# Batched one-hot comparisons in a graph kernel, and the basis product spread anew over its steps

## Chip, cores and metric

The kernel runs on one core of a Trainium2 chip. The metric is the device time of one execution in microseconds (us); less is better. A profile of one execution stands beside the timed runs; its span is a little shorter than the time of its own run.

## What is computed

625 nodes with 512 features pass through two graph blocks. The first is a graph convolution with batch norm, an exact GELU and a residual, then a layer norm; the second is a relational convolution of two layers with two relations, whose weights are sums over 30 basis matrices, then a residual and a layer norm. The edge list has 20,625 entries (src, dst, type), sorted by dst.

```python
# block 0: x -> layernorm(x + gelu(batch_norm(A_norm @ (x @ W0.T) + b0)) + x)
xw = x @ W.T
deg = segment_sum(ones_like(row), col)          # row, col: the edges and one loop for each node
dinv = where(deg > 0, rsqrt(deg), 0)
out = segment_sum((dinv[row] * dinv[col])[:, None] * xw[row], col) + b
# block 1: x -> layernorm(x + layer2(relu(layer1(x))))
def rgcn_gate_layer(x, row, col, edge_type, basis, att, gate_w, root, bias):
    w = einsum('rb,bio->rio', att, basis)       # basis: 30 x 512 x 512, fp32
    x_j = x[col]
    msgs[r] = (sigmoid(x_j @ gate_w[r]) * x_j) @ w[r]
    agg = segment_sum(where(edge_type == 0, msgs[0], msgs[1]), row)
    return agg + x @ root + bias
```

## The kernel before

All five engines run programs written out by hand, in program order, tied by semaphores; there is no scheduler. Products in fp32 precision are made of an upper and a lower part of each operand (`mm3`, three products at L476 to L478).

**The adjacency.** The edges are cut into 162 tiles of 128 edges, in 27 groups of 6. For a tile, `oh_src` (128 edges x place within a chunk of 125 nodes) and `oh_key` (128 edges x 160: five chunks, two relations, 16 columns of a window of destinations) are one-hot matrices, and TensorE multiplies them into `psE` (L570), three tiles to a window. VectorE makes the 162 `oh_key` (L1047) and 54 of the `oh_src` (L1045), one instruction for each tile with a scalar per edge; ScalarE makes the other 108 `oh_src` in two steps (L785, L791). VectorE then adds each of the 54 windows onto `B` (`add_window`, L1038) at a column that it reads from memory into a register (L1032). Group g waits on TensorE until the windows of group g - 2 are added, since `psE` has two halves. This loop over groups runs from 13.8 to 95.2 us. Behind it `AT` (B summed over relations, with the self loops added: L1103, L1105), the degrees (L601), `dinv`, and `z` (`xw` scaled, in two parts: L824, L1117) follow, then the aggregation `agg0` (L623) in eight steps (four blocks of 128 features, two halves of the nodes), batch norm and GELU by feature block, transposes back (`g`, L642), `residual_sum` (L1170) and layer norm, transposes of x1 (L650), the product with `root1`, then the gates, `Z` and `h` of each layer.

**The first product and the basis product in between.** `xw_part` (x @ W0.T) has 20 steps of three products; in the loop, groups 4 to 13 do two steps each. The combined weights are made from 64 basis parts (`basis_part`, L495), 32 for each layer. A part is four products of 128x32 by 128x512 on one slot of `basis_ring`, which has four slots of 1 MB; SP loads part n + 4 when part n has been used (L383). `basis_upto(n)` lets TensorE do the parts, in pairs, up to n. Eight parts make one block of weights (pp = 0 to 7), and each block goes through `w_first` (ScalarE, psW to `half`, L764, after part 8 pp + 3), `w_merge` (VectorE, L1011 to L1015, after part 8 pp + 7), `w_high` (ScalarE, L780) and `w_low` (VectorE, L1027). TensorE may not start part 8 pp + 8 before `w_first(pp)`, nor part 8 pp + 12 before `w_merge(pp)`. The numbers of parts done by places, before the change: 24 when the loop ends, 26 before `agg0`, 34 before the transposes `g`, 38 before `root1`, 46 after `root1`, 60 after Z of layer 1, 64 within `h`.

**Around the loop.** `w_merge(0)` stands at group 11, `w_low(0)` at 14, `w_merge(1)` at 20, `w_low(1)` at 23; `w_merge(2)` between `AT` and the degrees, `w_low(2)` in the third feature block of batch norm, `w_merge(3)` in the layer norm after the second chunk. `turned_low` (L1002) splits the nine transposed blocks of x and W0 in groups 1 to 5. `diag` (L1113) is made on VectorE and broadcast by TensorE (L611) into `dinv_b`, which VectorE copies (L1122).

## Time and profile before

| what | value |
|---|---|
| median of three runs | 326.71 us (326.15 to 327.0) |
| time of the profiled execution | 326.88 us |
| its span in the profile | 325.0 us |
| TensorE busy | 283.5 us, 87% |
| VectorE busy | 175.3 us, 54% |
| ScalarE busy | 135.3 us, 42% |
| GpSimd busy | 36.5 us, 11% |
| mean granted TensorE clock | 0.94 of full |
| moved by DMA | 73.7 MB |

Read with care: a matmul counts as busy until its modelled end, and the shares are averages over stages with different limits. Durations of consecutive VectorE instructions overlap a little, so that the distance of their starts is what an instruction costs in a row of them.

### The profile page before, as it was taken

To read this page: it belongs to the slowest core of one execution; us is meant where nothing else is said; L and a number is where in the kernel's file an instruction comes from. 1 tells how busy PE (TensorE), PEld (TensorE's weight loads), DVE (VectorE), ACT (ScalarE), POOL (GpSimd) and SP (SyncE) were. 2 spreads that over 40 slices of the span, in tenths; PEclk is the share of its full clock that TensorE was granted. 3 is DMA by queue.
4 is the path that set the end of the run, shared out by engine and by line. 5 is a ranking of instruction groups with operands and counts; after the bars stand their busy time and mean duration, and the time that the engine had idled before them with its cause. 6 is when DMAs were issued, how large, how long until landed. Compare 5 with 4: busy or idle time off the path is not lost.

```text
span 325.0 us, 4963 instructions
## 1 busy us (share of the span) xinstructions
PE 283.5 (87%) x1711; PEld 193.4 (60%) x1711; DVE 175.3 (54%) x538; ACT 135.3 (42%) x265; POOL 36.5 (11%) x71
## 2 busy tenths in 40 slices
PE   1768899885969999568999999999997999999991
PEld 1653455432336786424767656647795777787771
DVE  3878787999967847686310132233325125433333
ACT  4596868899701368647243114111313142100000
POOL 1001000000002900551000000000003600010000
PEclk9987999998695999779999999999998999999997
DMA  6974869599997999739998677975001400001112
GB/s 175 335 327 158 336 257 356 207 388 416 352 385 282 314 354 418 313 103 367 382 381 318 260 292 303 418 294 246 2 0 32 132 0 0 2 0 33 33 34 63
DMA packets 12759, 73.68 MB, mean 227 GB/s; under 512 B 1952, under 2 KB 2195, under 8 KB 4540
## 3 DMA queue, kind: packets, MB, share of 16 engines
q1 hardware_dynamic: 11282, 70.82, 57.4%
q0 software_dynamic: 1104, 2.36, 2.8%
q10 hardware_dynamic: 346, 0.17, 0.3%
q8 instruction: 14, 0.23, 0.3%
q14 instruction: 13, 0.11, 0.1%
HBM read 72.05 MB, written 1.28 MB: 226 GB/s over the span
## 4 chain that ended last, share of the span: by engine, by line
PE 61%; DVE 22%; issue 7%; DMA 4%; DVEq 2%; ACT 1%; POOL 1%; ACTq 0%; POOLq 0%
PE psW L495 13%; PE psM L476 10%; PE psM L477 9%; PE psM L478 9%; PE psM L717 6%; PE psM L737 6%; DVE oh_key L1047 4%; DMA basis_ring<-in_L_gnn_basis_dram 3%; PE psM L623 3%; DVE B L1038 2%; PE psE L570 2%; DVEq L1032 2%; DVE w L1027 1%; DVE x_sum L1170 1%; DVE AT L1103 1%
## 5 line engine op out<-in xcount | busy, mean ns | idle before, releaser
L495 PE MATMUL psW<-basis_ring,S 128*32 128x512 f32 x512 | 68.2, 651 | 3.2 <-DMA basis_ring<-in_L_gnn_basis_dram 3.1
L1217 DVE SCALAR_TENSOR_TENSOR zg<-psM,gate,zg 125x512 fp32r<-125x512 f32 x20 | 15.0, 751 | 59.5 <-ACT zg L891 59.5
L1047 DVE TENSOR_SCALAR oh_key<-iota_f,key 128x160 f16<-128x160 f16 x162 | 36.0, 262 | 2.6 <-PE psE L570 1.4
L785 ACT ACTIVATE oh_diff<-iota_f,edgeT 128x128 f16<-128x128 f16 x108 | 34.1, 389 | 3.4 <-DVEq L964 3.4
L495 PEld LDWEIGHTS psW<-basis_ring,S 128*32 128x32 f32 x512 | 13.9, 115 | 32.5 <-issue 26.4
L476 PE MATMUL psM<-w,hlT 128*125 128x512 f32 x80 | 33.1, 414 | 0.1
L891 ACT ACTIVATE zg<-psM,gate 125x512 fp32r<-125x512 f32 x20 | 13.8, 688 | 46.1 <-PE psM L478 45.7
L477 PE MATMUL psM<-w,hlT 128*125 128x512 f32 x80 | 32.3, 404 | 0.0
L478 PE MATMUL psM<-w,hlT 128*125 128x512 f32 x80 | 32.1, 402 | 0.0
L570 PEld LDWEIGHTS psE<-oh_key,oh_src 128*125 128x125 f16 x162 | 16.0, 150 | 25.2 <-issue 19.2
L570 PE MATMUL psE<-oh_key,oh_src 128*125 128x160 f16 x162 | 21.3, 261 | 10.2 <-issue 6.6
L717 PEld LDWEIGHTS psM<-BB,zg 125*128 125x128 f32 x160 | 23.1, 188 | 2.5 <-issue 1.7
L737 PE MATMUL psM<-zg,BB 125*125 125x512 f32 x100 | 24.0, 394 | 0.0
L717 PE MATMUL psM<-BB,zg 125*128 125x320 f32 (+1 forms) x160 | 23.8, 308 | 0.0
L791 ACT ACTIVATE oh_src<-oh_diff,ones_f 128x512 f16<-128x512 f16 x27 | 19.5, 722 | 7.1 <-PE psE L570 6.4
L737 PEld LDWEIGHTS psM<-zg,BB 125*125 125x125 f32 x100 | 18.6, 186 | 4.7
L1038 DVE TENSOR_TENSOR B<-B,psE 125x160 f32 x54 | 17.4, 322 | 6.8 <-issue 5.2
L476 PEld LDWEIGHTS psM<-w,hlT 128*125 128x125 f32 x80 | 15.1, 189 | 9.1 <-DVEq L1220 3.4
L460 POOL DMA_DIRECT2D root_raw<-in_L_gnn_root_dram x16 | 7.9, 501 | 101.0 <-DVE hlT L1243 101.0
L1027 DVE TENSOR_TENSOR w<-w_both,w 128x512 fp32r<-128x512 f32 x16 | 13.3, 869 | 9.9 <-ACT w L780 9.6
L478 PEld LDWEIGHTS psM<-w,hlT 128*125 128x125 f32 x80 | 15.3, 191 | 3.9
L477 PEld LDWEIGHTS psM<-w,hlT 128*125 128x125 f32 x80 | 15.3, 191 | 3.5
(159 smaller groups left out, 430.5 us busy)
## 6 DMA issues: line engine op xcount, KB each, us to landing
basis_ring<-in_L_gnn_basis_dram SPq DMA_DIRECT2D x64, 1024.0 KB, 7.1
root_raw<-in_L_gnn_root_dram POOLq DMA_DIRECT2D x32, 64.0 KB, 3.6
xs<-in_x_dram SPq DMA_DIRECT2D x1, 1120.0 KB
out_dram<-xs SPq DMA_DIRECT2D x5, 224.0 KB
w_raw<-in_L_gnn_W_dram SPq DMA_DIRECT2D x1, 1024.0 KB, 10.9
bias_b<-in_L_gnn_bias_dram POOLq DMA_DIRECT2D x1, 250.0 KB, 3.8
xs<-in_x_dram SPq DMA_DIRECT2D x1, 130.0 KB
out_dram<-xs SPq DMA_DIRECT2D x5, 26.0 KB
```

What stands on the lines that cost most here:

```text
L476: nc.tensor.matmul(o, l_hi, r_hi, start=start, stop=False)
L477: nc.tensor.matmul(o, l_hi, r_lo, start=False, stop=False)
L478: last[0] = nc.tensor.matmul(o, l_lo, r_hi, start=False, stop=stop)
L495: m = nc.tensor.matmul(psW[32 * j:32 * j + 32, cc % 2, :], S[:, cc % 2, cc // CH, q].rearrange("p k r -> p (k r)"), ring[:, n % RING, j, : ...
L570: nc.tensor.matmul(psE[0:PC, g % 2, at:at + KEYS], oh_src[:, g % 3, j * P:j * P + PC], oh_key[:, t % OH, :], start=(j % SG == 0), stop=(j ...
L717: last[0] = nc.tensor.matmul(bank(("h", f, h))[:, 0:n], zg[:, i, d, r, f * P:(f + 1) * P], BB[:, at:at + n], start=(d + r + i == 0), stop= ...
L737: last[0] = nc.tensor.matmul(bank(("out", c))[0:PC, :], BB[:, at:at + PC], zg[:, i, d, r, :], start=False, stop=(d == NC - 1 and r + i == 2))
L785: nc.scalar.activation(oh_diff[:, g % 3, j * P:(j + 1) * P], iota_f[:, 0:P], ACT.Abs, bias=edgeT[:, 0, g * G + j:g * G + j + 1], scale=-1. ...
L791: nc.scalar.activation(oh_src[:, g % 3, 0:GA * P], oh_diff[:, g % 3, :], ACT.Relu, bias=ones_f[:, 0:1], scale=-1.0).then_inc(src_ready, 1)
L1027: v.tensor_tensor(lo, full, hi, ALU.subtract).then_inc(w_lo, 1)
L1038: v.tensor_tensor(to, to, psE[0:PC, g % 2, h * KEYS:(h + 1) * KEYS] .rearrange("p (c t w) -> p c t w", c=NC, t=R), ALU.add).then_inc(win_a ...
L1047: v.tensor_scalar(oh_key[:, t % OH, :], iota_f[:, 0:KEYS], key[:, t:t + 1], None, ALU.is_equal) \
```

## The change

- **Comparisons in one instruction for six tiles.** `one_hots` compares a row of numbers with the edges' values laid out in pairs: each value stands twice, side by side (`place_pairs`, `key_pairs`, two casts before the loop), so that both inputs and the output are fp16 with an inner row of two. One instruction makes a group's six `oh_src` (6 x 126), one its six `oh_key` (960). ScalarE's share of `oh_src` is gone.
- **Register reads.** The two registers of a group's windows are read behind the two comparisons, and `add_window` follows for both windows of group g - 2.
- **Spreading.** In the loop, the xw steps run up to 2(g - 3)/3 and the basis parts up to 2g/3 - 2; 15 of the 20 steps and 16 parts lie in the loop, five steps behind it. The parts done are then 16 when the loop ends, 20 before `agg0`, 28 before `g`, 30 behind it, 36 before `root1`, 44 after `root1`, 58 after Z of layer 1, 64 within `h`.
- **The middle.** The self loops are written into `B` at the start by ScalarE and taken off the edge matrix again (`own_edge`) before `z_parts(0)`. `diag` is made by GpSimd, its broadcast products stand behind the first step of `agg0`, and ScalarE copies the result. `w_merge(1)` stands behind `z`, `w_low(1)` in the second feature block, `w_merge(2)` in the third, `w_low(2)` and `w_merge(3)` behind the first three chunks of x1, `w_high(2)` and `w_first(3)` ahead of the last GELU.
- **W0 in another row order.** W0 is loaded in four transfers so that h comes in the order of the basis product; the vectors are then needed in one order only.

```diff
-OH = 12
-GA = 4
+OH = 3 * G
+PLACES = PC + PC % 2
...
-        FIRST_XW = 4
+        PARTS_IN = 15
...
-        FIRST_AT = {8: 0, 17: 1}
-        HIGH_AT = {13: 0, 22: 1}
-        MERGE_AT = {11: 0, 20: 1}
-        LOW_AT = {14: 0, 23: 1}
+        MERGE_AT = {16: 0}
+        LOW_AT = {19: 0}
...
-            sp.dma_start(w0_raw[:], W0.rearrange("(c p) o -> p c o", p=P)).then_inc(w0_in, 16)
+            for j in range(JB):
+                sp.dma_start(w0_raw[32 * j:32 * j + 32], W0.rearrange("(k c j) o -> j k c o", k=2 * KB, c=KC)[j]) \
+                    .then_inc(w0_in, 16)
...
+            pool.wait_ge(dinv_ready, 1)
+            for c in range(NC):
+                nc.gpsimd.tensor_scalar(diag[:, c, :], ident[0:PC, 0:PC], dinv_p[:, c:c + 1], None, ALU.mult) \
+                    .then_inc(diag_ready, 1)
...
-                if FIRST_XW <= g < FIRST_XW + NC * KC // 2:
-                    xw_part(2 * (g - FIRST_XW))
-                    xw_part(2 * (g - FIRST_XW) + 1)
-                basis_upto(9 * g // 10)
+                xw_upto(2 * (g - 3) // 3)
+                basis_upto(min(2 * g // 3 - 2, PARTS_IN))
...
+            xw_upto(NC * KC)
             pe.wait_ge(vec_permuted, 1)
...
-            basis_upto(24)
...
-            basis_upto(25)
...
-            basis_upto(26)
+            basis_upto(17)
+
+            basis_upto(19)
...
+                    if (f, h) == (0, 0):
+                        pe.wait_ge(diag_ready, NC)
+                        for i, (c0, c1) in enumerate(((0, 4), (4, NC))):
...
-                basis_upto((28, 30, 31, 32)[f])
-            basis_upto(33)
+                basis_upto((21, 23, 25, 27)[f])
...
+            basis_upto(29)
...
-                basis_upto((35, 36, 37)[c])
+                basis_upto((31, 33, 35)[c])
...
-                    basis_upto(39 + KC * h + f)
+                    basis_upto((37, 37, 39, 39, 41, 41, 43, 43)[KC * h + f])
...
-                            basis_upto(47 + 7 * (R * c + r) // 5)
+                            basis_upto((45, 47, 47, 49, 51, 51, 53, 55, 55, 57)[R * c + r])
...
-                    basis_upto(min(60 + KC * h + f, 2 * CH * SUB - 1))
+                    basis_upto((57, 59, 59, 61, 61, 63, 63, 63)[KC * h + f])
...
+            def one_hots(out, pairs, first, n, width):
+
+                pair = iota_f[:, 0:width].rearrange("p (k i) -> p k i", i=2)
+                shape = [P, n, width // 2, 2]
+                return v.tensor_tensor(out, pair.unsqueeze(1).broadcast_to(shape),
+                                       pairs[:, first:first + n].unsqueeze(2).broadcast_to(shape), ALU.is_equal)
...
-                link(v.tensor_tensor(AT[:, c], B[:, c, 0, 0:N2], B[:, c, 1, 0:N2], ALU.add))
-                d = AT[:, c, c * PC:(c + 1) * PC]
-                v.tensor_tensor(d, d.bitcast(F32), ident[0:PC, 0:PC], ALU.add).then_inc(at_ready, 1)
-            w_merge(2)
+                v.tensor_tensor(AT[:, c], B[:, c, 0, 0:N2], B[:, c, 1, 0:N2], ALU.add).then_inc(at_ready, 1)
...
+            w_merge(1)
+            dve.wait_ge(dinv_b_ready, 2)
...
-                if f == 2:
-                    w_low(2)
...
+                if f == 1:
+                    w_low(1)
+                if f == 2:
+                    w_merge(2)
...
-                if c == 1:
-                    w_merge(3)
...
-            w_low(3)
+            w_low(2)
+            w_merge(3)
```

VectorE in the middle of the loop, the instructions of one group. Before (`TENSOR_LOAD` reads a window's register):

```order
L1045 TENSOR_SCALAR oh_src<-iota_f,edgeT 128x128
L1047 TENSOR_SCALAR oh_key<-iota_f,key 128x160
L1045 TENSOR_SCALAR oh_src<-iota_f,edgeT 128x128
L1047 TENSOR_SCALAR oh_key<-iota_f,key 128x160 x3
L1032 TENSOR_LOAD base_i
L1032 ISA x2
L1038 ISA
L1038 TENSOR_TENSOR B<-B,psE 125x10x16
L1047 TENSOR_SCALAR oh_key<-iota_f,key 128x160 x2
L1032 TENSOR_LOAD base_i
```

After, on the same engine at the same place:

```order
L1055 TENSOR_TENSOR oh_src<-iota_f,place_pairs 128x6x126
L1038 TENSOR_LOAD base_i
L1038 ISA x2
L1055 TENSOR_TENSOR oh_key<-iota_f,key_pairs 128x960
L1038 TENSOR_LOAD base_i
L1038 ISA x2
L1048 ISA
L1048 TENSOR_TENSOR B<-B,psE 125x10x16
L1048 ISA
L1048 TENSOR_TENSOR B<-B,psE 125x10x16
```

Eight comparisons have become two, and no comparison stands between the two windows any more.

TensorE in the loop, before (one group with two xw steps and a pair of parts, and the start of the next):

```order
L570 MATMUL psE<-oh_key,oh_src 125x160 x6
L476 MATMUL psM<-w0T_hi,xT_hi 125x512
L477 MATMUL psM<-w0T_lo,xT_hi 125x512
L478 MATMUL psM<-w0T_hi,xT_lo 125x512
L476 MATMUL psM<-w0T_hi,xT_hi 125x512
L477 MATMUL psM<-w0T_lo,xT_hi 125x512
L478 MATMUL psM<-w0T_hi,xT_lo 125x512
L495 MATMUL psW<-basis_ring,S 32x512 x8
L570 MATMUL psE<-oh_key,oh_src 125x160 x6
```

After, on TensorE, three groups:

```order
L580 MATMUL psE<-oh_key,oh_src 125x160 x12
L479 MATMUL psM<-w0T_hi,xT_hi 125x512
L480 MATMUL psM<-w0T_lo,xT_hi 125x512
L481 MATMUL psM<-w0T_hi,xT_lo 125x512
L498 MATMUL psW<-basis_ring,S 32x512 x8
L580 MATMUL psE<-oh_key,oh_src 125x160 x6
L479 MATMUL psM<-w0T_hi,xT_hi 125x512
L480 MATMUL psM<-w0T_lo,xT_hi 125x512
L481 MATMUL psM<-w0T_hi,xT_lo 125x512
```

Three groups now carry two xw steps and one pair of parts; before, two groups carried four steps and one pair.

VectorE behind the loop, before and after:

```order
L1103 TENSOR_TENSOR AT<-B 125x626
L1105 TENSOR_TENSOR AT<-AT,ident 125x125
L1011 SCALAR_TENSOR_TENSOR w_both<-psW,mask_h,w_half 128x512
L1013 SCALAR_TENSOR_TENSOR w_half<-psW,mask_h,w_half 128x512
L1015 STREAM_SHUFFLE w_both<-w_half 128x512
L1108 COPY deg<-psM 125x5
L1113 TENSOR_SCALAR diag<-ident,dinv_p 125x125 x5
L1117 SCALAR_TENSOR_TENSOR z<-xw,dinv_p,z 125x512 x5
```

```order
L1121 TENSOR_TENSOR AT<-B 125x626 x5
L1123 COPY deg<-psM 125x5
L1129 SCALAR_TENSOR_TENSOR z<-xw,dinv_p,z 125x512 x5
L1018 SCALAR_TENSOR_TENSOR w_both<-psW,mask_h,w_half 128x512
L1020 SCALAR_TENSOR_TENSOR w_half<-psW,mask_h,w_half 128x512
L1022 STREAM_SHUFFLE w_both<-w_half 128x512
```

The first two rows of before stand five times in turn; a `w_merge` that stood ahead of the copy of the degrees now stands behind `z`, and `diag` has left the engine.

## Rows read from the trace of the kernel before

**Rows 1.** Busy time by stretch: us, busy by engine, granted clock, DMA share, GB/s

```profile
13.80:37.20 23.40, 18.65 (x113) 12.08 (x112) 18.82 (x76) 19.32 (x49) 1.04 (x1) 0.85 0.69 267
37.20:62.40 25.20, 22.88 (x153) 13.69 (x152) 20.73 (x96) 20.68 (x49) 0.00 (x0) 1.00 0.82 317
62.40:95.20 32.80, 25.17 (x193) 10.42 (x193) 29.70 (x137) 23.75 (x57) 0.00 (x0) 0.90 0.92 356
...
95.00:101.00 6.00, 5.16 (x30) 5.13 (x30) 5.64 (x11) 0.22 (x1) 0.00 (x0) 0.62 0.99 418
...
138.00:146.00 8.00, 5.14 (x28) 1.84 (x28) 7.17 (x19) 3.40 (x5) 4.17 (x9) 0.79 0.29 92
...
149.70:172.70 23.00, 23.00 (x168) 16.46 (x169) 7.17 (x12) 8.85 (x17) 0.00 (x0) 1.00 0.98 376
172.70:217.00 44.30, 44.30 (x252) 26.91 (x253) 10.19 (x15) 11.62 (x19) 0.00 (x0) 1.00 0.78 307
```

**Rows 2.** Groups of instructions by line: count, busy us, mean ns, idle before

```profile
L1047 DVE TENSOR_SCALAR oh_key<-iota_f,key 128x160 f16<-128x160 f16 x162 | 36.0, 262 | 2.6 <-PE psE L570 1.4 <-DVE xT_lo L1002 0.7 <-DVE w0T_lo L1002 0.2
...
L1038 DVE TENSOR_TENSOR B<-B,psE 125x160 f32 x54 | 17.4, 322 | 6.8 <-issue 5.2 <-DVE B L1038 1.4
...
L1045 DVE TENSOR_SCALAR oh_src<-iota_f,edgeT 128x128 f16<-128x128 f16 x54 | 13.5, 250 | 0.6 <-DVE w_both L1015 0.5
...
L1103 DVE TENSOR_TENSOR AT<-B 125x626 fp32r<-125x626 uint16 x5 | 4.0, 806 | 0.9 <-DVE B L1038 0.9
```

**Rows 3.** Timeline of VectorE within the loop: start us, duration us

```profile
65.48 0.26 DVE L1045 TENSOR_SCALAR oh_src<-iota_f,edgeT 128x128 f16<-128x128 f16 x1
...
67.29 0.26 DVE L1045 TENSOR_SCALAR oh_src<-iota_f,edgeT 128x128 f16<-128x128 f16 x1
...
75.03 0.74 DVE L1011 SCALAR_TENSOR_TENSOR w_both<-psW,mask_h,w_half 128x512 f32<-128x512 f32 x1
...
77.46 0.26 DVE L1045 TENSOR_SCALAR oh_src<-iota_f,edgeT 128x128 f16<-128x128 f16 x1 [0.25 <-DVE w_both L1015]
...
83.26 1.95 DVE L1027 TENSOR_TENSOR w<-w_both,w 128x512 fp32r<-128x512 f32 x2
85.13 0.24 DVE L1045 TENSOR_SCALAR oh_src<-iota_f,edgeT 128x128 f16<-128x128 f16 x1
```

**Rows 4.** Timeline of VectorE at the end of the loop

```profile
93.97 0.33 DVE L1038 TENSOR_TENSOR B<-B,psE 125x160 f32 x1 [0.43 <-DVE B L1038]
95.19 0.81 DVE L1103 TENSOR_TENSOR AT<-B 125x626 fp32r<-125x626 uint16 x1 [0.89 <-DVE B L1038]
...
96.24 0.80 DVE L1103 TENSOR_TENSOR AT<-B 125x626 fp32r<-125x626 uint16 x1
```

**Rows 5.** Timeline of TensorE: a group of the loop, and the broadcast of dinv

```profile
45.35 0.58 PE L570 MATMUL psE<-oh_key,oh_src 128*125 128x160 f16 x6
...
47.28 1.92 PE L495 MATMUL psW<-basis_ring,S 128*32 128x512 f32 x16
49.14 0.63 PE L570 MATMUL psE<-oh_key,oh_src 128*125 128x160 f16 x6
...
105.59 1.88 PE L611 MATMUL psM<-diag,ones_f 125*128 125x125 f32 x10 [0.17 <-DVE diag L1113]
```

**Rows 6.** The chain that ended last, in order of time: start us, us

```profile
100.42 0.75 DVE w_both L1011
...
103.23 1.21 POOL dinv_p L430
104.47 1.06 DVE diag L1113 x5
105.53 3.32 DVE z L1117 x5
108.90 1.98 PE psM L623 x12
...
133.01 0.72 PE psM L642 x4
...
149.67 0.39 PE psM L476
```

More of the change, by code:

```diff
@@ L255, in gnn_block @@
         use("deg", "dve")
-        for h in range(2):
-            use(("dinv", h), "dve")
         NBB = -(-NC * R * NC // 4)
@@ L562, in _ @@
             for g in range(NG):
[L563 removed]
+                pe.wait_ge(key_ready, g + 1)
                 if g >= 2:
@@ L1058, in _ @@
[L1058 to L1063 removed]
+                    dve.wait_ge(b_zero, NC)
+                for i in TURNED_LOW_AT.get(g, ()):
+                    turned_low(i)
+                for i, w in enumerate(range(2 * (g - 2), 2 * (g - 1)) if g >= 2 else ()):
+                    add_window(w, at[i])
@@ L1112, in _ @@
             for c in range(NC):
-                last = v.tensor_scalar(diag[:, c, :], ident[0:PC, 0:PC], dinv_p[:, c:c + 1], None, ALU.mult)
-            last.then_inc(diag_ready, 1)
-            for c in range(NC):
                 dve.wait_ge(z_hi, c + 1)
@@ L1229, in z_parts @@
                             .then_inc(root_ready, 1)
+            for d in range(NC):
+                own_edge = BB[:, d * (R * NC + 1) * PC:(d * (R * NC + 1) + 1) * PC]
+                last = v.tensor_tensor(own_edge, own_edge.bitcast(F32), ident[0:PC, 0:PC], ALU.subtract)
+            link(last)
             z_parts(0)
```

165 lines of the change are left out of this document (80 added, 85 removed).

## Prediction

> **What bounds the kernel now.** I read the stretches first [rows 1]. A reader should see three regimes. In the loop, 13.8 to 95.2 us, no engine is full: VectorE is busy for 18.8 + 20.7 + 29.7 = 69.3 of 81.4 us, TensorE for 66.7. From 149.7 to 217 TensorE is busy without a gap, and up to 172.7 the DMA share is 0.98 too. Between them the limit passes from one engine to another: at 138 to 146 us DMA is busy for 0.29 of the time, since the ring is full and TensorE uses no parts. The costliest groups [rows 2] and the timeline [rows 3] then give the loop's prices. Starts of two like instructions are 1.81 us apart (65.48, 67.29): that is a group's bill on VectorE. A window lasts 0.32, but instructions in a row overlap by about 0.08 (the `w_low` from 83.26 lasts 1.95 and the next starts at 85.13), so it costs 0.24; two of them leave 1.34 us for the six keys and two places. TensorE [rows 5]: six adjacency products and two xw steps take 1.93 us (45.35 to 47.28), a pair of basis parts 1.86 (47.28 to 49.14). In groups 4 to 13, two groups with one pair cost TensorE 2 x 1.93 + 1.86 = 5.7 us against 3.6 on VectorE; later VectorE is the longer one. The two take turns, and nobody gets the sum of both evened out. That is what the spreading attacks.
>
> **The loop.** Removed: 162 + 54 comparisons on VectorE (1.34 us a group). Added: one of 756 elements and one of 960 a group. The trace has no two-input VectorE instruction with fp16 alone. Upper bound, the two-input rows: 160 elements take 322 ns, 626 take 806 [rows 2], so 1.04 ns an element and 156 ns fixed; the two take 0.94 + 1.15 less two overlaps = 1.92 us. Lower bound, the one-input fp16 rows: 128 columns take 250 ns and 160 take 262, 0.38 ns an element; that gives 0.78 us. I take half the upper bound's rate, 0.52 ns, because the inputs are two-byte as in the lower row and two as in the upper: 0.55 + 0.65 - 0.17 = 1.03 us.
> The Trainium skill (VectorE: DVE Perf Modes, section on the perf-mode tier table) says that a tensor_tensor gives two results a cycle where all operands are 16-bit with unit step in SBUF, and one otherwise; no run here shows it yet. By it the sum would be the 1.03, and the 1.92 if the broadcast pairs did not count as unit step.
> The rest, against 95.2 us, the start of `AT` [rows 4]:
> - two casts ahead of the first key, 324 outputs each at the upper rate: +0.8;
> - 27 groups x (1.34 - 1.03): -8.4;
> - the second window stands directly behind the first and has to wait for its end: 0.46 in place of 0.24, 25 times: +5.5. The register reads now run while a comparison of half a microsecond is worked on;
> - one `w_merge` (75.03 to 77.46, 2.43) and one `w_low` (83.26 to 85.13, 1.87) leave the loop [rows 3]: -4.3;
> - VectorE's idle time is 81.4 - 69.3 = 12.1 us. The last four windows and the read of `more` keep 2.2 (0.43 and 0.89 are shown in [rows 4]), the waits of nine `turned_low` on themselves another 2.2 (0.25 each). Of the other 7.7, which were waits for TensorE's bursts, for ScalarE's places and for register reads (5.2 of the 6.8 at L1038 [rows 2]), I keep 1.2: -6.5.
> Sum -12.9: `AT` starts at about 82.3 us; call it L. TensorE doesn't forbid it: three groups cost it 1.2 + 1.5 + 1.86 = 4.6 us (three times 0.4, two steps, a pair) against 3 x 1.73 = 5.2 on VectorE. ScalarE, busy for 19.3 + 20.7 + 23.8 = 63.8 us there [rows 1], loses the places, most of that, and so will be ready before it is asked. ScalarE's five copies onto B and the W0 load in four transfers I cost at nothing: the first hide before the first window, the second behind the first comparisons; if W0 came late, the first adjacency product, which stands behind a W0 transpose on TensorE, would move with it one for one.
>
> **From L to the end of root1.** Before, this took 95.2 to 172.7, 77.5 us. Eight parts fewer are done by L, and six of them must be done in this stretch. Two paths run through it, and the later one counts.
> *Engines.* Before the degrees' copy VectorE loses a 2.4 us `w_merge` (100.42, [rows 6]) and five adds (96.24 - 95.19 = 1.05 a chunk, 0.72 without). TensorE, though, has five xw steps to do first (3.6 us) and 25 small products; I expect the copy 4.8 us behind L, 7.6 before. The 1.06 us of `diag` leave the path (104.47), but z's lower part now waits 0.7 for the first upper part. z is then ready at L + 10.5, before at 108.90 - 95.19 = 13.7: -3.2. The broadcast products, 1.88 us with half-clock products among them [rows 5], stood under VectorE's z and now stand on TensorE behind the first `agg0` step: +1.6. `w_low(1)`, `w_merge(2)` and the steps ahead of the last GELU replace one `w_low` of equal size: 0. `w_merge(3)` leaves the layer norm, 2.4 us: -2.4 (133.01 to 149.67). Together 77.5 - 4.0 = 73.5.
> *Transfers.* Parts 16 to 19 are in the ring at L and are used behind the degree products, from L + 4.8 on. Part 20 can be asked for at L + 5.7 and lands at about L + 10.3. A part is 1.05 MB: 2.5 us at the best rate seen (418 GB/s, 95 to 101), 2.8 at that of 149.7 to 172.7 (376); I take 2.65. Root1 (1 MB) shares the stretch, 3 us. Part 43, the last before the gates, lands at L + 10.3 + 3 + 23 x 2.65 = L + 74.3; its product and the last `root1` block add 0.9 + 1.8: L + 77.
> So the transfers rule, and the 4 us gained on the engines buy only 0.5. Before, the ring had idled through 138 to 146; the six parts now use just that hole, and the transfers are late instead of the layer norm. At 2.5 us a part the engines' 73.5 would rule, at 2.8 it is L + 80.5.
>
> **From root1 on.** 14 parts in Z of layer 1 as before; six in `h` in place of four, where TensorE is full: one pair, +1.9. `own_edge` (five adds of about 0.3 us) runs while VectorE waits for the gates: 0. The bubble of the last `w_merge(7)` stays.
>
> **Sum.** 326.9 (the profiled execution, within 0.2 of the median) - 12.9 - 0.5 + 1.9 = 315.4 us.
>
> **Rivals.**
> *A, the comparisons run at one element a cycle.* For it: a row of two with a broadcast around it is no plain run, and every two-input row here runs at 1.04 ns. Then a group costs 0.89 us more, 27 groups 24 us, L = 106.3; with -0.5 + 1.9 the time is 339 us, slower than before. It decides from 1.03 + 11.5 / 27 = 1.46 us for the two. Against: the whole layout in pairs makes inner rows of two-byte neighbours. By the skill's rule named above this is the case if the step of such a row does not count as one. Chance 0.07.
> *B, the loop does not even out.* Group g of TensorE waits for both comparisons and both windows; in [rows 1] groups take 32.8 / 13 = 2.5 us late in the loop, and the clock is 0.85 and 0.90 where TensorE has gaps. If a group costs 2.05 instead of 1.78, 7 us come back: 322. Chance 0.14.
> *C, transfers slower than I take.* At 2.8 us and above a part in the middle, 319. Chance 0.14.
> *D, transfers no limit.* The engines' 73.5 rules: 312; with fewer stalls in the loop, 310. Chance 0.12.
> *The forecast*, 313 to 318: 0.53.
>
> **Chances.** A measurement of this kernel can tell 0.3%, 1 us, from no change. Slower than that: A, 0.07, and 0.01 from B gone wild. Within it 0.02. Faster 0.90. The range, 310 to 323, leaves out A and the tails of B and D, with what is left over less than 2 in 10.
>
> **What the profile after will show.** One instruction for six places of about 0.55 us and one for six keys of about 0.65 (A: 0.94 and 1.15); groups 1.7 to 1.8 us apart in the middle of the loop (B: over 2); `AT` starting near 82; TensorE's clock near 1 there. z ready 10 to 11 us behind `AT`'s start. Then waits of TensorE for `basis_ring` between the x1 transposes and the end of root1, with the DMA share near 1 from about 95 to 155 us; without such waits D holds. The gates start 77 us behind `AT`. I am wrong on the loop if VectorE waits there for TensorE for over 3 us, and wrong on the middle if the parts land in time and yet 77 us pass.

## The result: slower by 1.4%, and where the profile after puts it

The changed kernel takes 331.62 us (median of four runs, 329.9 to 333.47) against 326.86 us before (four runs beside it, 326.15 to 328.33). The ratio is 1.0138, 95% interval 1.0097 to 1.0179: slower, where 315.4 us and a range of 310 to 323 were forecast. Measured a second time beside other experiments it was 332.69 (1.0155, 1.0092 to 1.0218). The profiled execution took 332.53 us, its span is 330.7.

The stretches of the kernel after. They answer to [rows 1]; each line ends with the granted clock, the DMA share and GB/s.

```profile
core 0: us, PE busy (x) PEld busy (x) DVE busy (x) ACT busy (x) POOL busy (x), PEclk, DMA share, GB/s
14.70:36.10 21.40, 11.57 (x64) 9.52 (x63) 16.90 (x41) 5.07 (x9) 1.05 (x1) 0.71 0.45 185
36.10:62.40 26.30, 21.77 (x160) 11.33 (x158) 21.19 (x53) 3.23 (x5) 0.00 (x0) 0.91 0.74 273
62.40:89.20 26.80, 20.38 (x150) 11.20 (x151) 20.19 (x48) 3.21 (x6) 0.00 (x0) 0.94 0.75 293
89.20:100.10 10.90, 10.90 (x73) 6.12 (x71) 6.44 (x10) 4.28 (x8) 4.63 (x6) 0.84 0.67 262
100.10:127.60 27.50, 24.27 (x196) 18.73 (x193) 17.04 (x48) 13.20 (x21) 9.93 (x20) 0.94 1.01 360
...
132.70:153.20 20.50, 14.68 (x97) 6.74 (x97) 15.86 (x35) 11.02 (x15) 9.64 (x14) 0.84 0.80 317
153.20:177.90 24.70, 24.70 (x170) 18.13 (x170) 8.02 (x17) 8.59 (x16) 0.00 (x0) 0.93 0.98 392
```

Three places stand on the timeline of every kernel: the first large comparison, the start of `AT`, and the start of the gates. Before they stood at 13.8, 95.2 and 172.7, of 325.0 us; after at 14.7, 89.2 and 177.9, of 330.7. So the loop became 6.9 us shorter (81.4 to 74.5), where 13 were forecast; the stretch from `AT` to the gates became 11.2 us longer (77.5 to 88.7; 7.5 longer in the profile of the second measurement), where 0.5 less was forecast; the rest, 152.3 us, is 152.8. The question is thus twofold: why half of the loop's gain is missing, and what took 7 to 11 us in the middle.

The middle of the loop on VectorE in the kernel after (start, duration, what, idle time ahead of it). It answers to [rows 3]; L1048 is a window, L1055 a batched comparison.

```profile
52.77 0.66 DVE L1055 TENSOR_TENSOR oh_key<-iota_f,key_pairs 128x960 f16<-128x960 f16 x1
53.60 0.78 DVE L1048 TENSOR_TENSOR B<-B,psE 125x160 f32 x2 [0.17 <-issue]
54.29 0.55 DVE L1055 TENSOR_TENSOR oh_src<-iota_f,place_pairs 128x756 f16<-128x756 f16 x1
54.76 0.66 DVE L1055 TENSOR_TENSOR oh_key<-iota_f,key_pairs 128x960 f16<-128x960 f16 x1
55.58 0.78 DVE L1048 TENSOR_TENSOR B<-B,psE 125x160 f32 x2 [0.17 <-issue]
```

Both comparisons cost what was forecast, 0.55 and 0.66 us. A group, though, takes 55.58 - 53.60 = 1.98 us and not 1.73: the first window starts 0.17 us after the 960-element comparison has ended, and "issue" says that the profile shows nothing that it waited for.

The middle on TensorE in the kernel after: the waits for `basis_ring` (in brackets), and the products behind the second and the last of them:

```profile
112.74 1.07 PE L498 MATMUL psW<-basis_ring,S 128*32 128x512 f32 x8 [0.55 <-DMA basis_ring<-in_L_gnn_basis_dram]
...
121.31 1.07 PE L498 MATMUL psW<-basis_ring,S 128*32 128x512 f32 x8 [2.45 <-DMA basis_ring<-in_L_gnn_basis_dram]
122.31 2.75 PE L623 MATMUL psM<-AT,z 125*128 125x320 f32 x10
...
145.04 1.06 PE L498 MATMUL psW<-basis_ring,S 128*32 128x512 f32 x8 [0.98 <-DMA basis_ring<-in_L_gnn_basis_dram]
...
148.82 1.06 PE L498 MATMUL psW<-basis_ring,S 128*32 128x512 f32 x8 [2.14 <-DMA basis_ring<-in_L_gnn_basis_dram]
151.27 1.93 PE L498 MATMUL psW<-basis_ring,S 128*32 128x512 f32 x8 [1.38 <-DMA basis_ring<-in_L_gnn_basis_dram]
153.13 0.64 PE L479 MATMUL psM<-hlT,root_hi 128*128 128x320 f32 x1
```

These are five waits, 7.5 us in sum. The `agg0` step at 122.31 takes 2.75 us where such a step otherwise takes 1.75, and from 150 to 155 us, behind the last two waits, the granted clock is 0.50, the lower of the two levels (1.2 of 2.4 GHz). The chain that ended last in the kernel after goes through the transfers at two places, which end with the waits of 2.45 and 1.38 us (start, duration, what):

```profile
107.20 14.07 DMA basis_ring<-in_L_gnn_basis_dram
...
142.55 8.68 DMA basis_ring<-in_L_gnn_basis_dram
```

And the DMA engines are not always busy. At 27 to 38 us the ring is full and nothing is moved; at 135 to 140 their share is 0.25:

```profile
27.00:38.00 11.00, 6.02 (x30) 4.46 (x28) 8.74 (x19) 1.76 (x3) 0.25 (x1) 0.50 0.00 0
...
135.00:140.00 5.00, 3.73 (x28) 2.11 (x27) 4.21 (x11) 2.39 (x3) 4.15 (x6) 0.87 0.25 62
150.00:155.00 5.00, 3.73 (x15) 2.07 (x16) 2.35 (x5) 3.31 (x4) 0.00 (x0) 0.50 1.01 428
```

### The profile page after: what moved, and what is told of

It is laid out like the page before. It is cut to its first block, busy times and chain, and to the rows that moved or that the text cites. A ratio compares the mean times of both kernels' runs of the same rounds, so it can differ in the third digit from the quotient of the medians.

```text
span 330.7 us, 4651 instructions
## 1 busy us (share of the span) xinstructions
PE 279.9 (85%) x1707; PEld 192.5 (58%) x1707; DVE 167.0 (50%) x371; ACT 87.4 (26%) x137; POOL 40.3 (12%) x76
## 4 chain that ended last, share of the span: by engine, by line
PE 65%; DVE 13%; DMA 8%; issue 6%; ACT 3%; POOL 2%; DVEq 2%; ACTq 0%; POOLq 0%
PE psW L498 15%; PE psM L479 11%; PE psM L481 9%; PE psM L480 9%; DMA basis_ring<-in_L_gnn_basis_dram 7%; PE psM L725 6%; PE psM L745 6%; DVE B L1048 3%; PE psE L580 3%; PE psM L623 2%; DVE oh_key L1055 2%; DVE oh_src L1055 1%; POOL root_lo L448 1%; DMA rows_i<-in_edge_type_dram 1%; DVEq L1038 1%
## 5 line engine op out<-in xcount | busy, mean ns | idle before, releaser
L498 PE MATMUL psW<-basis_ring,S 128*32 128x512 f32 x512 | 66.3, 634 | 7.5 <-DMA basis_ring<-in_L_gnn_basis_dram 7.5
L580 PE MATMUL psE<-oh_key,oh_src 128*125 128x160 f16 x162 | 19.2, 265 | 20.3 <-DVE B L1048 20.2
L479 PE MATMUL psM<-w,hlT 128*125 128x512 f32 x80 | 32.5, 406 | 0.1
L481 PE MATMUL psM<-w,hlT 128*125 128x512 f32 x80 | 31.7, 396 | 0.0
L480 PE MATMUL psM<-w,hlT 128*125 128x512 f32 x80 | 31.6, 395 | 0.0
L896 ACT ACTIVATE zg<-psM,gate 125x512 fp32r<-125x512 f32 x20 | 13.8, 688 | 46.3 <-PE psM L481 45.9
L1048 DVE TENSOR_TENSOR B<-B,psE 125x160 f32 x54 | 17.5, 323 | 11.4 <-PE psE L580 2.7
L479 PEld LDWEIGHTS psM<-w,hlT 128*125 128x125 f32 x80 | 14.8, 185 | 8.9 <-issue 2.5
L1055 DVE TENSOR_TENSOR oh_key<-iota_f,key_pairs 128x960 f16<-128x960 f16 x27 | 17.7, 655 | 1.1 <-issue 0.9
L772 ACT ACTIVATE w_half<-psW,mask_h 128x512 f32<-128x512 f32 x16 | 10.0, 679 | 29.7 <-PE psW L498 29.4
L481 PEld LDWEIGHTS psM<-w,hlT 128*125 128x125 f32 x80 | 14.8, 185 | 3.9
L480 PEld LDWEIGHTS psM<-w,hlT 128*125 128x125 f32 x80 | 14.8, 185 | 3.4
L1055 DVE TENSOR_TENSOR oh_src<-iota_f,place_pairs 128x756 f16<-128x756 f16 x27 | 14.8, 547 | 1.1 <-DVE xT_lo L1008 0.7
```

The lines of the kernel that those rows point to most:

```text
L479: nc.tensor.matmul(o, l_hi, r_hi, start=start, stop=False)
L480: nc.tensor.matmul(o, l_hi, r_lo, start=False, stop=False)
L481: last[0] = nc.tensor.matmul(o, l_lo, r_hi, start=False, stop=stop)
L498: m = nc.tensor.matmul(psW[32 * j:32 * j + 32, cc % 2, :], S[:, cc % 2, cc // CH, q].rearrange("p k r -> p (k r)"), ring[:, n % RING, j, : ...
L580: nc.tensor.matmul(psE[0:PC, g % 2, at:at + KEYS], oh_src[:, g % 3, j * P:j * P + PC], oh_key[:, t % OH, :], start=(j % SG == 0), stop=(j ...
L896: nc.scalar.activation(zg[:, 0, c, r, :], bank(("Z", L, c, r))[0:PC, :], ACT.Copy, scale=gate[:, L, c, r:r + 1]).then_inc(zg_hi, 1)
```

## The theories, and the stages of every kernel that ran

*Theory R (reads):* the missing part of the loop is VectorE's sequencer. A register read with its bounds instructions keeps it longer than the comparison in front lasts. *Theory S (spreading):* the eight parts put off into the middle make the ring's transfers the bound there, and each wait also halves the clock. *Rival E (engines):* the new order in the middle (`diag` on GpSimd, products behind the first `agg0` step, steps ahead of the last GELU) costs the time, and the waits for the ring only fill gaps.

All experiments below change the kernel after. Each ratio is to the kernel before run beside it, whose median was 326.55 to 328.41 us; a difference of two times from different rounds is thus good to 1 or 2 us only. The stages in the table, in us, come from one profiled execution of each kernel; n is the number of parts in the loop.

| kernel | n | first comparison | `AT` starts | loop | `AT` to g | g to gates | gates to end |
|---|---|---|---|---|---|---|---|
| before | 24 | 13.8 | 95.2 | 81.4 | 37.8 | 39.7 | 152.3 |
| after | 16 | 14.7 | 89.2 | 74.5 | 43.6 | 45.1 | 152.8 |
| after, again | 16 | 16.6 | 91.6 | 75.0 | 42.8 | 42.2 | 154.4 |
| e1 old spreading | 24 | 17.8 | 97.1 | 79.3 | 38.7 | 39.8 | 150.8 |
| e2 half the bytes | 16 | 14.2 | 88.4 | 74.2 | 38.7 | 39.8 | 152.9 |
| e3 GELU first | 16 | 16.7 | 91.2 | 74.5 | 45.6 | 47.2 | 153.0 |
| e4 windows first | 16 | 14.4 | 89.7 | 75.3 | 40.7 | 43.9 | 152.9 |
| e5 one read | 16 | 14.7 | 83.5 | 68.8 | 43.8 | 43.8 | 152.8 |
| e6 = e1 + reads | 24 | 15.9 | 90.2 | 74.3 | 40.9 | 40.1 | 150.7 |
| e7 twenty parts | 20 | 15.7 | 90.8 | 75.1 | 38.9 | 42.1 | 154.4 |
| e8 = e6, xw even | 24 | 14.8 | 85.0 | 70.2 | 39.2 | 39.8 | 150.7 |
| e9 = e7 + reads | 20 | 14.8 | 77.9 | 63.1 | 39.3 | 41.6 | 152.9 |
| e10 = after + reads | 16 | 14.9 | 79.1 | 64.2 | 45.7 | 43.3 | 152.9 |
| e11 a quarter of root1 | 16 | 14.6 | 89.0 | 74.4 | 38.7 | 43.8 | 152.9 |

The instructions ahead of the first comparison are the same in all rows behind the first; 14.2 to 17.8 us there is what executions of one program differ by at the start, so the columns of stages are the ones to compare. The profiled execution isn't the median one: for e2 and e9 it was the fastest (322.36 and 313.47), for e3 the slowest.

TensorE's waits for the ring between `AT` and the gates follow the number of parts in the loop: 6.2 to 8.9 us with 16 parts (after twice, e3, e4, e5, e10), 3.8 and 3.3 with 20 (e7, e9), 0 and 0.4 with 24 (e1, e8), none before.

## Experiments

### e1: the old spreading with everything else new

```diff
-                xw_upto(2 * (g - 3) // 3)
-                basis_upto(min(2 * g // 3 - 2, PARTS_IN))
+                xw_upto(min(max(2 * (g - FIRST_XW + 1), 0), NC * KC))
+                basis_upto(9 * g // 10)
...
-        MERGE_AT = {16: 0}
-        LOW_AT = {19: 0}
+        MERGE_AT = {11: 0, 20: 1}
+        LOW_AT = {14: 0, 23: 1}
```

> The kernel after with the spreading undone: 24 parts and all 20 xw steps at the groups where the kernel before has them, and the parts, w_first, w_high, w_merge and w_low behind the loop at its places too. Batched comparisons, register reads, self loops in B, diag on GpSimd and the late dinv copy stay. Theory S (the eight parts put off make the transfers the bound of the middle, and the early groups' loss is in the loop): AT starts near 90 us with 24 parts behind it instead of 16, waits for basis_ring behind it fall under 2 us, the gates come 77 us or less behind AT, and the time is 317 to 322 us, faster than both. Rival M (the new order of the middle, with diag on GpSimd and the products behind the first agg0 step, costs the time): the time stays at 328 us or above.

325.55 us, ratio to before 0.9961 (0.993 to 0.9991). `AT` to gates falls from 88.7 to 78.5 us, and no wait for the ring is left in it. `diag` on GpSimd and the products behind the first `agg0` step are still there, so they aren't what costs the time. They aren't a gain either, since before took 77.5. Two things differ besides the transfers, though: TensorE has six parts fewer in this stretch, and the steps of the combined weights stand at their old places, so that rival E's third item, the steps ahead of the last GELU, isn't tested here. e2 and e3 do that. The time I expected, 317 to 322, was too good: the loop took 79.3 us, since VectorE has two `w_merge` and two `w_low` in it and a group costs 1.98 us there as well. And of the batched comparisons, in a loop with the same work as before, 2.1 us are left.

### e2: half the bytes of the later parts

```diff
-                sp.dma_start(ring[:, n % RING].rearrange("p j o -> p (j o)"), rows[c // 2, c % 2]) \
+                width = JB * D // (2 if n >= 16 else 1)
+                sp.dma_start(ring[:, n % RING].rearrange("p j o -> p (j o)")[:, 0:width], rows[c // 2, c % 2][:, 0:width]) \
```

> The kernel after, but from part 16 on a load brings only the first half of a part's bytes (half of each row; the other half of the slot keeps old values, so the combined weights are not the reference's). All instructions of the engines stay. Theory S: the 7 to 9 us of waits for basis_ring between AT and the gates vanish, with the half clock behind each; the first root1 block starts near 148.5 instead of 153.2 and the time is 321 to 324 us. Rival E (the engines' order is the bound, transfers only fill the gaps): under 2 us gained, 330 us or more.

324.72 us, ratio 0.9946 (0.9908 to 0.9983) to before, so 7 us less than the kernel after. No instruction of an engine differs, and `AT` to gates is 78.5 us with 1.1 us of waits for the ring left. This shows theory S: with the transfers nearly out of the way the engines need 78.5 us, and 10.2 us of the 88.7 (6.5 of the 85.0 in the second profile) are the transfers' doing. That e1 took 78.5 too is a coincidence, since it has six parts fewer there. It also shows that rival D (transfers no limit) would not have given 73.5; more on this below.

### e3: the last GELU ahead of w_high(2) and w_first(3)

```diff
-                if f == KC:
-                    w_high(2)
-                    w_first(3)
                 if f:
                     act.wait_ge(bn_ready, f)
...
+                if f == KC:
+                    w_high(2)
+                    w_first(3)
```

> The kernel after with w_high(2) and w_first(3) on ScalarE behind the last GELU instead of ahead of it. Theory S: the GELU starts about 1.3 us earlier, but parts 33 to 35 land no earlier, so the time changes by less than 0.5 us, 331 to 332. Rival E: the 1.3 us come through to the end, 330.

336.15 us, ratio to before 1.0239 (1.0187 to 1.029): neither theory, it got slower by 4.5 us (3.3 by the ratios). The profiled execution was 338.76, above its three others, 333.44 to 336.35. ScalarE and GpSimd behind the last GELU in e3, and then the same chain in the kernel after:

```profile
135.85 0.91 ACT L842 ACTIVATE hf<-hf,bn 128x625 f32<-128x625 f32 x1 [1.57 <-DVE bn L1141]
136.66 2.09 ACT L788 ACTIVATE w<-w_both 128x512 fp32r<-128x512 f32 x2
138.65 1.23 ACT L772 ACTIVATE w_half<-psW,mask_h 128x512 f32<-128x512 f32 x2
139.79 3.98 ACT L850 ACTIVATE root_hi<-root_raw 128x512 fp32r<-128x512 f32 x4
146.29 1.53 ACT L862 ACTIVATE xs<-x_sum,lnm,lrs 125x512 f32<-125x512 f32 x2 [2.52 <-POOL lnm L456]
...
140.94 4.48 POOL L448 TENSOR_TENSOR root_lo<-root_raw,root_hi 128x512 fp32r<-128x512 f32 x3 [5.79 <-ACT root_hi L850]
145.39 0.54 POOL L455 TENSOR_TENSOR lrs<-lrs,mhalf 125x1 f32<-125x1 f32 x1
```

```profile
131.80 0.90 ACT L845 ACTIVATE hf<-hf,bn 128x625 f32<-128x625 f32 x1
132.60 3.98 ACT L850 ACTIVATE root_hi<-root_raw 128x512 fp32r<-128x512 f32 x4
139.12 0.81 ACT L862 ACTIVATE xs<-x_sum,lnm,lrs 125x512 f32<-125x512 f32 x1 [2.55 <-POOL lnm L456]
...
133.74 4.51 POOL L448 TENSOR_TENSOR root_lo<-root_raw,root_hi 128x512 fp32r<-128x512 f32 x3 [4.02 <-ACT root_hi L850]
138.22 0.54 POOL L455 TENSOR_TENSOR lrs<-lrs,mhalf 125x1 f32<-125x1 f32 x1
```

What is moved behind the GELU stands ahead of `root_hi`. GpSimd has three `root_lo` (4.5 us) to do before the inverse root of the first chunk, and these wait for `root_hi`. So the first normalised chunk comes 146.29 - 135.85 = 10.4 us behind the GELU in place of 7.3. Of the two places tried, the two steps cost less ahead of the GELU. What this experiment doesn't explain is `AT` to g, 45.6 against 43.6 and 42.8, with the same program up to there: waits for the ring of 1.98 and 3.24 us, in place of 0.55 and 2.45.

### e4: windows ahead of turned_low

```diff
-                for i in TURNED_LOW_AT.get(g, ()):
-                    turned_low(i)
                 for i, w in enumerate(range(2 * (g - 2), 2 * (g - 1)) if g >= 2 else ()):
                     add_window(w, at[i])
+                for i in TURNED_LOW_AT.get(g, ()):
+                    turned_low(i)
```

> The kernel after with the two windows of a group ahead of turned_low in groups 2 to 5 instead of behind it. TensorE waits 20 us for windows in the loop, 4.3 of it at 25 us. Theory: these waits in the early groups fall by 2 to 4 us in sum, the first basis pair starts 1 to 3 us earlier than 38.1, and AT starts 0.5 to 2 us earlier than 89.2; the time falls by as much or less, 329.5 to 331.5. Rival: the early groups' pace is set by the sum of VectorE's work, and nothing moves, 331.6.

330.07 us, ratio 1.0118 (1.0054 to 1.0182); its interval overlaps that of the kernel after, and that the time lies in my range says nothing for the theory, since the loop didn't move. It took 75.3 us and isn't shorter, and TensorE still waits 19.7 us for windows (20.2 in the kernel after). My theory on the early groups is wrong, and the result is the rival's: the order within a group moves nothing. That VectorE's sum of work sets the pace there is argued, not shown by itself.

### e5: one register read for both windows

```diff
-                at = [window_at(2 * (g - 2))] if g >= 2 else []
+                at = window_at(2 * (g - 2), 2) if g >= 2 else []
...
-                if g >= 2:
-                    at.append(window_at(2 * (g - 2) + 1))
```

`window_at` now loads two neighbouring numbers with one instruction, without the two bounds instructions behind each load.

> The kernel after with one register read for both windows of a group, between the two comparisons, and without the two bounds instructions that each read brings; nothing else changes. Theory R (the 0.17 us before each first window and the 0.28 now and then before oh_key are VectorE's sequencer, which needs some 0.75 us for a read and its bounds): a group in the middle of the loop falls from 1.98 to 1.73 us on VectorE, AT starts 3 to 6 us earlier than 89.2, and of that at least 2 us reach the end, so 326 to 330. Rival (the gap belongs to the window itself, by its register address or its wait for TensorE): group 1.98, time 331.6.

324.5 us, ratio to before 0.9891 (0.985 to 0.9931), 7 us below the kernel after (8 by the ratios), and below the 326 to 330 that I expected. VectorE in the middle of the loop:

```profile
52.55 0.55 DVE L1058 TENSOR_TENSOR oh_src<-iota_f,place_pairs 128x756 f16<-128x756 f16 x1
53.02 0.65 DVE L1058 TENSOR_TENSOR oh_key<-iota_f,key_pairs 128x960 f16<-128x960 f16 x1
53.59 0.76 DVE L1051 TENSOR_TENSOR B<-B,psE 125x160 f32 x2
54.27 0.54 DVE L1058 TENSOR_TENSOR oh_src<-iota_f,place_pairs 128x756 f16<-128x756 f16 x1
54.73 0.65 DVE L1058 TENSOR_TENSOR oh_key<-iota_f,key_pairs 128x960 f16<-128x960 f16 x1
55.30 0.77 DVE L1051 TENSOR_TENSOR B<-B,psE 125x160 f32 x2
```

No gap is left, and a group takes 55.30 - 53.59 = 1.71 us. The same window instructions, with registers as addresses and the same wait for TensorE, now follow without a gap, so the rival is out and theory R is shown. The profile of e1 says the same without any change to the reads: where VectorE had a `w_low` of 1.97 us queued ahead (62.56), the next first window started 0.56 us after its comparison's start (64.90, 65.46) and had no gap. With the gap gone the loop takes 68.8 us against the 68.5 of the sum (82.3 - 13.8). The trace has the reads themselves (engine DVEq is VectorE's sequencer; count, then ns min/median/max, first and last start). In the kernel after, and then in e5:

```profile
L1038 DVEq TENSOR_LOAD <-base_i x54: 299/301/549, 20.8 to 86.9; - x54
L1038 DVEq FUSED_REGOPS  x54: 183/190/200, 21.4 to 87.2; - x54
L1038 DVEq SEQ_ASSERT  x54: 23/23/35, 21.6 to 87.4; - x54
```

```profile
L1038 DVEq TENSOR_LOAD <-base_i x29: 303/526/772, 20.8 to 81.5; - x29
```

In the kernel after the loads of one group start at 52.14 and 52.80: a read with its bounds instructions takes the sequencer 0.66 us, and the second one ends at 53.4, when the comparison (52.77 to 53.43) is nearly done; the window's own address work and its start at 53.60 follow. One load of two numbers takes 0.53 us and has no bounds instructions behind it. From the start of the first load to that of the first window it is thus 1.46 us in the kernel after (52.14 to 53.60) and 1.21 in e5 (52.38 to 53.59), where the comparison and no longer the sequencer comes last. An estimate from these rows: of 1.32 us for two reads the bounds instructions are 0.66, and joining the two loads saves 0.1. The middle stays at 87.6 us: here an earlier `AT` moves it as a whole.

### e6 to e10: how many parts the loop should hold

Reads a group ahead, and the two windows of a group apart, so that the second needn't wait for the first:

```diff
+                if g >= 2:
+                    add_window(2 * (g - 2), at[0])
                 one_hots(oh_key[:, g * G % OH:g * G % OH + G]...
                     .then_inc(key_ready, 1)
+                if g >= 1:
+                    at_next = window_at(2 * (g - 1), 2)
...
+                    add_window(2 * (g - 2) + 1, at[1])
```

e6 puts this (from group 6 on) on e1's spreading, e8 does so in every group and spreads the xw steps evenly with `xw_upto(9 * (g - 3) // 10)`; e7 is the kernel after with `basis_upto(min(4 * g // 5 - 1, 19))` alone, e9 is e7 with the reads, e10 the kernel after with the reads.

> The kernel with the old spreading (e1), with one read for both windows, a group ahead and behind oh_key, and from group 6 on the first window between oh_src and oh_key, the second behind oh_key, so that neither waits for the other. Theory R + S: a group on VectorE costs 0.46 + 0.24 + 0.57 + 0.24 = 1.5 us; VectorE saves 0.45 us a group over e1, TensorE (24 parts, 20 steps, 67 us of work) becomes the bound of the loop; AT starts 72 to 75 us behind the first oh_src instead of 79.3, and the time is 317 to 322. Rival: TensorE's waits and its clock eat the gain, 324 or more.

> The kernel after, but with 20 parts in the loop (up to 4g/5 - 1) instead of 16; behind the loop no more come before agg0, all else stays. Theory S: four loads more lie in the loop, where the DMA share is 0.74; the loop takes 0 to 3 us more, the waits for basis_ring behind it shrink from 7.5 us to under 3, AT to the gates falls from 88.7 to 80 to 84, and the time is 325 to 329. Rival E: the middle keeps its 88 us, and the time is 332 or more.

> One read for both windows, a group ahead, the windows apart in every group (as in e6_spread_reads, from group 2 on), 24 parts in the loop as in the kernel before, but the 20 xw steps spread evenly over groups 4 to 26 instead of two a group in 4 to 13. In e6_spread_reads VectorE waited 2.2 to 2.3 us at a time for TensorE's bursts. If the turns between the two engines cost the loop, AT starts 70 us behind the first oh_src (74.3 in e6_spread_reads) and the time is 317 to 320. Rival: TensorE's sum of work (67 us) and the waits for basis_ring bound it anyway, 322.

> The kernel of e7_twenty (20 parts in the loop, 15 xw steps) with one read for both windows, a group ahead, the windows apart in every group. Theory: VectorE costs 1.5 us a group, AT starts near 84 (90.8 in e7_twenty); the transfers, not the engines, set the way to the gates, so that less than half of these 6 us is left there, and the time is 320 to 324. Rival (engines set it): all 6 us are left, under 320.

> The kernel after (16 parts in the loop) with one read for both windows, a group ahead, the windows apart in every group. Against e5_read a group saves another 0.22 us. Theory S: AT starts 78 to 80 (83.5 in e5_read), but the waits for basis_ring grow, the gates stay within 2 us of 171, and the time is 322 to 325, no better than e5_read by more than 2 us. Rival: the time falls by the whole 4 to 5 us, 320.

| parts in the loop | slow reads | new reads |
|---|---|---|
| 16 | after 331.62 (1.0138, 1.0097 to 1.0179) | e10 323.74 (0.9896, 0.9803 to 0.9988) |
| 20 | e7 326.41 (0.9921, 0.9887 to 0.9955) | e9 317.64 (0.9706, 0.9617 to 0.9795) |
| 24, steps in 4 to 13 | e1 325.55 (0.9961, 0.993 to 0.9991) | e6 322.61 (0.9807, 0.9727 to 0.9888) |
| 24, steps even | not run | e8 316.52 (0.964, 0.9558 to 0.9723) |

Four parts more in the loop cost it nothing (e7 75.1 against 74.5, e9 63.1 against 64.2) and take 5 us and more off the time, since `AT` to gates falls from 84.6 to 92.8 us (the six profiles with 16 whole parts in the loop and the whole of root1) to 81. The loop of the kernel after had the room: its DMA share was 0.75, and VectorE bound it. In e9's quicker loop the share is 1.00 to 1.01 from 35 us on, so this room is used up there. For e7 I had expected waits for the ring under 3 us; they were 3.8.

From e5 to e10 the loop gains 4.6 us and the time 0.8, in the range that theory S gave, with waits of 8.9 us in place of 7.3. But the two profiles show only 1.4 us more between `AT` and the gates (the gates come at 168.1, not within 2 us of 171), so how much of a quicker loop is lost there with 16 parts isn't settled. With 20 parts it is not lost: e9's loop gains 12.0 us over e7, `AT` to gates is the same (80.9 and 81.0), and the time falls by 8.8. I had expected 320 to 324 and less than half of the gain left; 317.64 is where the rival put it, and the transfers do not set e9's way to the gates as I thought.

e6, at 322.61 us just above the 317 to 322 that I expected, shows rival B's mechanism once VectorE is quick. VectorE in e6, and the wait for TensorE's two xw steps and a pair of parts:

```profile
43.61 0.32 DVE L1048 TENSOR_TENSOR B<-B,psE 125x160 f32 x1 [2.29 <-PE psE L580]
...
49.31 0.32 DVE L1048 TENSOR_TENSOR B<-B,psE 125x160 f32 x1 [2.27 <-PE psE L580]
```

A group costs 1.5 us of VectorE when nothing is waited for, and TensorE's bursts take it back. e8 takes 4.1 us less in the loop with the same work, and its 316.52 us is a little below the range of 317 to 320. Two things changed there, the even steps and the windows apart from group 2 on in place of group 6, and no run parts them. e8 and e9 beat both kernels; their intervals overlap. In e9 the waits that are left show the pace of the transfers. TensorE in e9, ahead of root1:

```profile
129.07 1.07 PE L498 MATMUL psW<-basis_ring,S 128*32 128x512 f32 x8 [0.50 <-DMA basis_ring<-in_L_gnn_basis_dram]
...
131.56 1.07 PE L498 MATMUL psW<-basis_ring,S 128*32 128x512 f32 x8 [0.85 <-DMA basis_ring<-in_L_gnn_basis_dram]
134.04 1.07 PE L498 MATMUL psW<-basis_ring,S 128*32 128x512 f32 x8 [1.42 <-DMA basis_ring<-in_L_gnn_basis_dram]
```

One part in 2.48 to 2.49 us: undisturbed, the ring is quicker than the 2.65 that I took.

### e11 and e12: a quarter of root1, and the kernel after beside it

```diff
+            link(nc.gpsimd.memset(root1_raw[:], 0.0))
             for kc in range(KC):
-                for j in range(JB):
+                for j in range(1):
```

> The kernel after, but GpSimd clears root1's buffer and only 4 of the 16 transfers of root1 are made, so that root1 is not the reference's. While root1's sixteen transfers of 64 KB run (about 104 to 120 us) the trace shows 307 to 324 GB/s at a share of 1, and 400 to 428 elsewhere. If root1 costs the ring more than its own 1 MB (my sum took 3 us), the waits for basis_ring at 112 to 121 us vanish and the way from AT to the gates falls from 88.7 by 5 us or more, the time to 326 or less. If it costs only its bytes: 2 us or less, 329.5 to 331.

> The kernel after, unchanged, beside e11 on the same chip, since its first four runs spread over 329.9 to 333.5. Both theories: 330 to 333 us.

328.25 us for e11 (1.0043, 1.0011 to 1.0076) against 332.69 for the kernel after in the same comparison: 4.4 us for 0.79 MB, which at the ring's pace of 2.49 us for 1.05 MB would be 1.9. The time lies between the two forecasts. `AT` to gates is 82.5 us, 6.2 less than in the first profile of the kernel after and 2.5 less than in the second, so that root1 costs the ring more than its bytes, by an amount that these runs give only roughly. The same 8 us in both, the kernel after (first profile) ahead of e11:

```profile
112.00:120.00 8.00, 6.31 (x56) 4.29 (x52) 6.13 (x19) 6.98 (x10) 1.10 (x2) 1.00 1.02 327
```

```profile
112.00:120.00 8.00, 8.00 (x72) 5.64 (x61) 6.83 (x20) 6.74 (x9) 1.10 (x2) 1.00 1.01 418
```

The queues are as busy in both and move a fifth less in the first; in e11 the four transfers of root1 that are left are over by 112 us. In the kernel after the parts move 4.2 MB from 104 to 120 us, which at 418 GB/s would take 10 us: by this estimate the whole of root1 costs the ring 6 us. The waits at 112 and 121 us are gone, and `AT` to g is 38.7, that of e1 and e2. The Trainium skill (Perfetto Trace Analysis, section DMA Optimizations) says that transfers under 2 KB have a significant overhead each, and that making 4 or 8 KB of 2 KB can help much. root1's rows have 2 KB (64 KB a transfer, against 1024 KB of a part in rows of 8 KB), and the two rates go the same way; but root1 is also issued by GpSimd on another queue than the parts, and no run here changes the size or the queue alone.

## Why the prediction was wrong, step by step

- **The comparisons: right.** 0.55 and 0.65 us forecast, 547 and 656 ns measured (median of 27 each). Rival A is dead. From 756 to 960 elements this is 109 ns for 204, 0.53 ns each, half the 1.04 ns of the fp32 rows. The Trainium skill (VectorE: DVE Perf Modes, section on the perf-mode tier table) has two results a cycle for a 16-bit tensor_tensor in SBUF where fp32 has one; by the 0.53 and 1.04 ns the trace agrees, also where a row of two is repeated by a broadcast.
- **The register reads: the step that failed in the loop.** "The register reads now run while a comparison of half a microsecond is worked on" priced them at nothing, though the trace of before has them in the same sizes (0.30 us for a load at L1032, 0.18 and 0.02 for its bounds instructions). Two reads with their two bounds instructions each outlast the comparisons, which shows as 0.17 us of idle time ahead of the first window and a lost overlap of 0.08; a group costs 1.98 and not 1.73 us, 25 x 0.25 = 6.3 us, where the loop missed its forecast by 6.0 (74.5 and not 68.5 us). e5 shows it. My own alarm, VectorE waiting for TensorE for over 3 us, stayed silent at 2.7 us, since the wait was for the sequencer. The rest of the loop's sum (merges, idle time, second window at 0.46) came out to 0.3 us in e5 as a whole; its terms were not taken one by one.
- **Rival B had the loop's loss about right (2.05 us a group, 7 us) and the mechanism wrong.** That its size came close is luck: TensorE's turns weren't it until e6 made VectorE quick.
- **The engines' path, 73.5 us: 5 too low.** e2, without the transfers' limit, took 78.5. Up to g it is 38.7 where the sum gives 37.8 - 3.2 + 1.6 = 36.2. I had anchored on z. The copy of the degrees came 5.8 us behind `AT` and not 4.8, and z was complete at 101.2, 12.1 behind `AT` and not 10.5 (before 13.7): 1.6 gained and not 3.2. TensorE does parts 16 to 19 on the way, in 5.3 us and not 3.7 (94.86 to 100.2 in the kernel after, in a stretch whose clock is 0.84), so that `agg0` starts 10.9 us behind `AT`, before 12.0, a gain of 1.1. From g to the gates it is 39.8 where 39.7 - 2.4 = 37.3 was forecast. `w_merge(3)` did leave the layer norm, but TensorE now has eight parts between g and root1 in place of four, 3.7 us more by the price of a pair, which I hadn't counted; that these are what is late there is read from this sum, and no run takes it apart.
- **The transfers' path, 77 us: the mechanism right, the size 8 to 12 too low.** The waits came where they were forecast, between the x1 transposes and root1, but also in `agg0`. **The step that failed in the middle is this sum.** Part 35 was used at 151.27, 62.1 us behind `AT`; the sum gives 10.3 + 3 + 15 x 2.65 = 53.1. Two terms fell. Root1 was taken at its own bytes' rate, 3 us, but three quarters of it cost 4.4, and by the estimate under e11 the whole costs 6. And "the six parts now use just that hole" is false: no part is used from 129.5 to 136.8 us, while TensorE waits for the last GELU and makes the transposes g, the ring's four slots fill, and the DMA share is 0.25 at 135 to 140 us, with parts 33 to 35 late ten microseconds after. That share leaves 3.7 of 5 us unused. The sum of parts times their duration has no place for a full ring. Of the 9 us at part 35 these two make 6 to 7 by this estimate; the rest isn't taken apart.
- **The clock behind the waits wasn't priced.** The `agg0` step at 122.31 (2.75 for 1.75), the part at 151.27 (1.93 for 1.07) and the first block of root1 (153.13 to 156.50, 3.4 for 1.9) give back 3.4 us. With 7.5 us of waits against e2's 1.1 this comes to 9.8, near the 10.2 us; it is a sum of rows and not an experiment. But not every wait is followed by half a clock: behind those of 0.55 and 0.98 us it stayed whole. And in the second profile of the kernel after the last wait ahead of root1, of nearly the same length, though with a shorter one before it (0.83 in place of 2.14 us), had the full clock behind it:

```profile
151.80 1.07 PE L498 MATMUL psW<-basis_ring,S 128*32 128x512 f32 x8 [1.41 <-DMA basis_ring<-in_L_gnn_basis_dram]
152.80 0.41 PE L479 MATMUL psM<-hlT,root_hi 128*128 128x320 f32 x1
```

  The granted clock was 1.00 there, and the first block of root1 took 1.9 us. These 2.3 us are most of the 2.9 by which g to gates differs between the two profiles (45.1 and 42.2).
- **From root1 on: +1.9 forecast, +0.5 measured.** The pair was priced right, and something else became quicker. With 16 or 20 parts in the loop the gates are 152.8 to 154.4 us from the end, with 24 parts 150.7 to 150.8: the extra pair costs 2. Against before it was only +0.5, since the new kernels need 1.5 less there at equal spreading (152.3 before, 150.8 in e1); what gives these 1.5 wasn't looked for. `own_edge` at nothing: nothing in these sums contradicts it, and no run isolates it.
- **Rival C (transfers slower, 319) had the mechanism, at 0.14, and a price of a part (2.8 us) that isn't what was wrong.** The rival that was missing is the one that happened: the loop half as good *and* the parts put off costing 10 us.
- **Other signs that were named.** TensorE's clock in the loop was to be near 1 and was 0.71, 0.91 and 0.94; the DMA share was to be near 1 from 95 to 155 us and was 0.67 up to 100.1 and 0.80 from 132.7 to 153.2. The waits for the ring between the x1 transposes and root1 did come.

What stays open: the middle with 16 parts took from 84.6 to 89.0 us in five profiles with the same instructions behind `AT` (after twice, e4, e5, e10). The clock is part of it, as shown above; what moves the waits for the ring from one execution to the next, the runs here don't settle. So the 10.2 us stand for one profile: by the profiles it is 6 to 10, by the times 7.
